# Second half of the gating at steps 1 and 2 of the next chunk; norms and input statistics at other steps

## The chip, the cores and the metric

The kernel runs on one core of a Trainium2 chip. The metric is the device time of one execution in microseconds. Engines run side by side, each takes its own instructions in order, and they meet only at semaphores: TensorE (PE, with PEld for its weight loads), VectorE (DVE), ScalarE (ACT), GpSimd (POOL), and SyncE (SP), which issues most of the transfers.

## The reference

For `x` of 8 x 64 x 56 x 56 floats:

```
x = x + conv3x3(groupnorm32(x))
t = tokens of x                       # 3136 tokens of 64 channels for each image
t = t + softmax(q k^T / 8) v          # q, k, v are linear maps of layernorm(t)
l = layernorm(t) @ gate_w + gate_b    # 16 experts
top 2 of softmax(l), renormalised     # two gates for each token
t = t + sum over the two experts of gate * (silu(h w1) * (h w2)) w3, h = layernorm(t)
```

## The kernel before, in words

**Tiling.** An image is cut into 7 chunks of 448 tokens, 56 chunks in all, numbered n = 0 to 55; c = n mod 7 is the place in the image. The queries of a chunk meet all 3136 keys of its image in 25 steps of 128 keys. One pass through `body(at)` is one chunk: each engine walks the same 25 steps and at each step issues its share. The order is written out by hand in tables of step numbers; there is no planner. So a step is a place in each engine's own queue and no moment in time: an engine can be steps behind another, held only by semaphores.

**What a chunk holds.** In each step PE makes the scores (L1463, L1464, two matmuls), ACT their exponential (L951), and PE weighs the values with it in groups of four or five (L1475: five pairs of halves at step 1, four at 5, 9, 13, 17, 21). Beside that three other chunks are in work: the one a whole image ahead ("pre": group norm, convolution L1501, tokens, layer norm `norm1`/`apply1`, keys), the one just attended ("post", chunk n-1: output projection, `attended`, layer norm `norm2`/`apply2`, transposes L1547, gate matmul L1554, `logits`, gating), and experts of an earlier image ("experts", `gated` on DVE).

**The maxima.** PE also computes the next chunk's scores once, only for their maxima ("passes", L1435, 21 or 28 of them in a chunk), and DVE reduces each (L1116). The passes go round two PSUM buffers, so pass m waits until DVE has reduced pass m-2 (`max_red`). The table `max_passes` gives most steps one pass, steps 2 (and 3 for c = 6) two where c is 1, 3, 5 or 6, and steps 0 to 4 two each where c is 0. DVE issues the reduces of a step first, then the entries of `STEPS` in order, then the combines, the experts, and `next_queries` (q_b, step 9).

**The gating** of the post chunk has two halves. The first: transposes (11), gate matmul (12), `logits` (13: add of the bias and four top-8 searches). The second: `picked` (step 16: four index searches L1183, one subtract L1184), `compared` (17: L1189 and two compares L1191), `gate_exp` on ACT (17, L894), `gates` (18: L1201 to L1203). Where c = 0 (and at chunk 53) the image's or group's routing starts at step 18 of the same chunk and needs all picks.

**Input statistics.** For the group norm of the image two ahead, SP loads a chunk of `x` into the only buffer `x_st` (L594, two halves, semaphore `x_st_in`), as the first thing in its `body` for the chunk, after the last things of the body before: the store of the experts' results (L620), which waits for the last result of that chunk (`fy_ready`). DVE waits for `x_st_in` and takes the statistics (`stats`, L1039) at step 9. This runs for n = 0 to 41; in the last chunk of an image the aggregation L1045 follows.

**POOL** makes both `rstd` powers at its steps `NORM2_AT` and `NORM1_AT`, between indirect DMAs.

Of the kernel before, what the change touches and what calls it, by code (L numbers as in the profile page):

```python
# [16 lines left out]
CHUNKS = TOKENS // CHUNK  # L17
# [59 lines left out]
def fx_loads(e, part):  # L77
# [21 lines left out]
COMBINES = {4: ((1, 0),), 5: ((0, 1), (1, 2)), 6: ((0, 3), (1, 4)), 8: ((0, 5), (1, 6))}  # L99
COMBINES_LAST = {4: ((1, 0),), 5: ((0, 1), (1, 2)), 6: ((0, 3), (1, 4)), 7: ((0, 5),), 8: ((0, 6),)}  # L100
GATHERS = {4: (0, 1), 5: (2, 3), 6: (4, 5), 7: (6,)}
NORM2_AT, NORM1_AT, RSTD_AT = 7, 11, 14
MOVES_AT = {4: (13, 16, 19, 22), 8: (1, 4, 8, 12, 15, 17, 19, 21), 9: (1, 4, 8, 11, 13, 15, 17, 19, 21),
            10: (0, 2, 4, 8, 12, 14, 16, 18, 20, 22)}
MOVES_AT_STORED = (4, 8, 12, 14, 16, 18, 20, 22)
# [7 lines left out]
SCATTERS_LAST = {GROUPS[-2].routed_at + 1: (0, 1), GROUPS[-2].routed_at + 2: (2, 3), ALL: (4, 5, 6)}  # L113
LAST = LATE + 2 * CHUNKS - 1
CONV_AT = 5
STEPS = [(4, "pre", "normed"), (4, "post", "attended"), (4, "post", "residual"), (6, "pre", "convolved"),
         (6, "post", "norm2"), (7, "pre", "tokens"), (8, "post", "apply2"), (9, "stats", "stats"), (10, "pre", "norm1"),
         (11, "post", "turned2"), (12, "post", "gate"), (13, "post", "logits"), (13, "stats", "mean"), (13, "stats", "deviation"),
         (14, "stats", "variance"), (14, "stats", "scale"), (14, "pre", "apply1"), (16, "post", "picked"), (17, "pre", "turned"),
         (17, "post", "compared"), (17, "post", "gate_exp"), (18, "post", "gates")]  # L120

# [64 lines left out]
def wait_past(engine, sem, value):  # L188

    if value > 0:  # L190
        engine.wait_ge(sem, value)
# [19 lines left out]
class At:  # L211
# [111 lines left out]
    def chunk(self, stage):  # L323

        if stage == "experts":
            return GROUP_SLICES[self.index("experts")][1]
        return self.index(stage) - CHUNKS * self.batch(stage)


def alone_pairs(at):  # L330
# [5 lines left out]
def expert_steps(at):  # L336

    if at.beside:
        return [(i, name, at, pair) for i, _, name, pair in EXPERT_STEPS
                if at.active("experts") and pair < at.pair_count()]  # L340
    if not at.active("experts"):
        return []
    steps, pairs = [], alone_pairs(at)
    here = [k for k, (mine, _) in enumerate(pairs) if mine.n == at.n]
    if here[-1] == len(pairs) - 1:
        here += [len(pairs) + k for k in range(3)]
    for place, k in enumerate(here):
        for name, behind in (("fx", 0), ("hidden", 1), ("gated", 1), ("down", 3), ("turn", 2)):
            if 0 <= k - behind < len(pairs):
                steps.append((at.steps() - KEY_TILES + 1 + 4 * place, name) + pairs[k - behind])  # L350
    return steps
# [13 lines left out]
def build(nc, x, conv_w, wq, bq, wk, bk, wv, bv, gate_w, gate_b, w1, w2, w3, out):  # L365
# [11 lines left out]
    with ctx:  # L377
        def sb(name, shape, dt=f32):
            return ctx.enter_context(nc.sbuf_tensor(name, shape, dt))
# [7 lines left out]
        before = sb("before", [TILE, TILE])  # L387
# [61 lines left out]
        gates = sb("gates", [TILE, 4, 2, TILES])  # L449
# [402 lines left out]
        def _(act):  # L852
# [55 lines left out]
            def expert(at, name, pair):  # L908
# [15 lines left out]
                elif name == "down":  # L924
                    act.wait_ge(s["y_done"], f + 1)
                    if pair == 0:
# [3 lines left out]
                                 (ps_z if at.beside else ps_m[1])[:, 0:2 * CHANNELS].rearrange("p (t c) -> p t c", c=CHANNELS),  # L930
                                 ACT.Copy, scale=0.5).then_inc(s["fy_ready"], 1)

            events = {"normed": normed, "tokens": tokens, "turned": turned,
                      "turned2": turned2, "gate_exp": gate_exp}

            def next_queries(n):
                act.wait_ge(s["q_done"], n + 1)
                a.activation(q_a[:, n % CHUNKS % QUERIES, :], ps_y[:, 0:CHUNK], ACT.Copy)\
                    .then_inc(s["qa_ready"], 1)

            def next_shift(n):
                wait_apart(act, s["shiftT_done"], n + 1)
                a.activation(q_a[0:1, n % CHUNKS % QUERIES, :], ps_y[0:1, 0:CHUNK], ACT.Copy)\
                    .then_inc(s["shift_ready"], 1)

            def body(at):
                experts = expert_steps(at)
                for i in range(at.steps()):
                    if at.attends:
                        act.wait_ge(s["s_done"], at.n * KEY_TILES + (i + 1))  # L950
                        a.activation(prob[(at.n * KEY_TILES + i) % PROBS][:], ps_s[(at.n * KEY_TILES + i) % 2][:, 0:CHUNK], ACT.Exp).then_inc(s["p_ready"], 1)  # L951
                    if i == Z_AFTER and at.active("post"):

                        act.wait_ge(s["pv_done"], (at.index("post") + 1) * KEY_TILES)
                        wait_past(act, s["outp_done"], at.index("post"))
                        a.activation(z_s[:], ps_o[:, 0:CHUNK], ACT.Copy).then_inc(s["z_ready"], 1)
                    for step, stage, name in STEPS:
                        if step == i and name in events and at.active(stage):
                            events[name](at)
                    for place, k in at.combines():  # L960
                        if i == at.combined_at(place):
                            combined(k)
                    for step, name, mine, pair in experts:
                        if step == i:
                            expert(mine, name, pair)
                    if i == at.ask_at and at.asks:
                        next_queries(at.n + 2)
                    if i == at.max_to + 1 and at.ahead:
                        next_shift(at.n + 1)
# [29 lines left out]
        def _(dve):  # L999
            v = nc.vector  # L1000

            def last_of_image(event):

                return lambda at: event(at.u + 2) if at.static and at.c == CHUNKS - 1 else None
# [288 lines left out]
            def combine(k):  # L1293
# [5 lines left out]
                for m in range(TOP):  # L1299
# [6 lines left out]

            events = {"normed": border, "convolved": conv, "norm1": norm1,
                      "apply1": apply1, "residual": attended, "norm2": norm2, "apply2": apply2,
                      "logits": logits, "picked": picked, "compared": compared,
                      "gates": gates_of,  # L1310
                      "stats": stats, "deviation": last_of_image(deviation), "scale": last_of_image(scale)}

            def body(at):
                b, coded = at.routes, CODES_AT.get(at.n)
                routes = b is not None
                codes_at = {4: 0, 5: 1, 9: 2, 13: 3, 17: 4} if coded is not None else {}
                maxima_at = max_passes(at) if at.ahead else ()
                codes_link = Link(dve, s["rt_link"], (coded or 0) * 25 + 12)
                link = Link(dve, s["rt_link"], (b or 0) * 25)
                experts = expert_steps(at)  # L1320
                for i in range(at.steps()):
                    for n, m in maxima_at[i] if at.ahead else ():
                        reduces(n, (m,))
                    for step, stage, name in STEPS:
                        if step == i and name in events and at.active(stage):
                            events[name](at)
                    for place, k in at.combines():
                        if i == at.combine_at(place):
                            combine(k)
                    for step, name, mine, pair in experts:  # L1330
                        if step == i:
                            expert(mine, name, pair)
                    if i in codes_at:
                        route_experts(coded, codes_link, codes_at[i])
                    if i == 3 and 1 <= at.n <= EXPERTS // 2:

                        expert_weights(at.n - 1)
                    if i == at.ask_at + 1 and at.asks:
                        next_queries(at.n + 2)
                    if i == at.max_to and at.ahead:  # L1340
                        max_total(at.n + 1)
                    if routes and i == 18:
                        route_pick(b)
                    if routes and i == 19:
                        route_total(b, link)
                    if routes and i == 20:
                        route_rank(b, link)
                    if routes and i == 21:
                        route_runs(b, link)
                        route_start(b, link)  # L1350
                    if routes and i == 22:
                        route_slot(b, link, 0)
                    if routes and i == 23:
                        route_slot(b, link, 1)
                    if routes and i == 24:
                        route_slots(b, link)
                assert not routes or link.count == 12, link.count
# [54 lines left out]
        def _(pe):  # L1412
# [243 lines left out]
            def body(at):  # L1656
# [18 lines left out]
                for i in range(at.steps()):  # L1675
# [16 lines left out]
                    if i == at.ask_at and at.asks:  # L1692
                        queries(at.n + 2, *divmod(at.n + 2, CHUNKS))
                    for step, stage, name in STEPS:
                        if step == i and name in events and at.active(stage):
# [90 lines left out]
```

## Time and profile before

| | us |
|---|---|
| median of 3 runs | 2696.83 (2693.95 to 2698.46) |
| the profiled execution | 2697.52 |
| its span, first to last instruction | 2695.8 |
| its mean granted TensorE clock | 0.963 |

A row of a timeline has the start, the busy time, the engine, the line and the tiles written and read; `x3` is three such instructions in a row, and what stands in brackets is idle time before and what ended it. The chunks spoken of below start, by their first score matmul, at 1084.79 (chunk 24), 1126.37 (25), 1259.91 (28), 1392.15 (31) and 1433.68 (32); chunk 33 starts at 1476.9. An image takes about 306.7 us in the middle of the run.

### The profile page before, as it was taken

The numbers are of one execution on the slowest core, as the hardware profiler recorded it, in microseconds if no ns is written. First come the engines' busy times: TensorE is split into PE (matmuls) and PEld (weight loads), VectorE is DVE, ScalarE is ACT, GpSimd is POOL, SyncE is SP. The second block draws the span as 40 slices with busy tenths as digits, with TensorE's granted clock in tenths as the row PEclk, the third lists the DMA queues.
The fourth block names the chain that finished last, engine by engine and source line by source line (L and its number), as shares of the span: only waits on it lengthen the run. The fifth ranks groups of instructions, "written<-read, shape, count | busy, mean of one in ns | idle before, by whom it ended". The sixth has DMA issues, their size and how long they took to land.

```text
span 2695.8 us, 46824 instructions
## 1 busy us (share of the span) xinstructions
PE 2443.3 (91%) x13821; PEld 1635.1 (61%) x13821; DVE 1804.3 (67%) x5891; ACT 1298.4 (48%) x2986; POOL 1012.8 (38%) x1097
## 2 busy tenths in 40 slices
PE   5899989999999999999999999999999999997773
PEld 3455555566666666666666666666666666664662
DVE  5576676667776777677766776677767777774432
ACT  2344444455554555455555555455555555453542
POOL 2022005300344424442444324443344324465765
PEclk8899999999999999999999999999999999997875
DMA  3143101111112222222222122222222112222442
GB/s 75 27 92 78 43 21 46 47 41 39 52 50 62 48 58 62 59 55 53 57 57 62 48 51 68 56 54 54 54 54 55 45 42 59 55 54 65 122 95 51
DMA packets 226560, 152.98 MB, mean 57 GB/s; under 512 B 100240, under 2 KB 216720, under 8 KB 226320
## 3 DMA queue, kind: packets, MB, share of 16 engines
q1 hardware_dynamic: 190880, 98.26, 14.0%
q0 software_dynamic: 31456, 48.03, 7.5%
q10 hardware_dynamic: 3984, 3.70, 0.5%
q8 instruction: 125, 2.05, 0.3%
q14 instruction: 115, 0.94, 0.1%
HBM read 83.92 MB, written 65.27 MB: 55 GB/s over the span
## 4 chain that ended last, share of the span: by engine, by line
PE 62%; DVE 17%; issue 5%; POOL 2%; ACT 1%; DMA 0%; POOLq 0%; ACTq 0%; DVEq 0%
PE ps_o L1475 17%; PE ps_m L1435 8%; PE ps_s L1463 7%; PE ps_s L1464 6%; DVE max_part L1116 5%; PE ps_z L1501 4%; PE ps_z L1648 3%; PE ps_x L1634 3%; PE ps_z L1623 2%; PE ps_s L1634 1%; PE ps_y L1538 1%; PE ps_y L1554 1%; DVE v_s L1029 1%; PE ps_y L1449 1%; PE ps_y L1562 1%
## 5 line engine op out<-in xcount | busy, mean ns | idle before, releaser
L1116 DVE TENSOR_REDUCE max_part<-ps_m 128x1 f32<-128x448 f32 x1400 | 845.1, 620 | 607.4 <-PE ps_m L1435 595.2
L951 ACT ACTIVATE prob<-ps_s 128x448 f32<-128x448 f32 x1400 | 758.7, 545 | 579.2 <-PE ps_s L1464 549.8
L1475 PE MATMUL ps_o<-prob,v_s 128*64 128x448 f32 x2800 | 622.1, 552 | 0.0
L1435 PE MATMUL ps_m<-k_a,q_a 128*128 128x448 f32 (+3 forms) x1600 | 540.1, 365 | 64.5 <-DVE max_part L1116 55.3
L1463 PE MATMUL ps_s<-q_a,k_a 128*128 128x448 f32 x1400 | 586.5, 419 | 2.4 <-ACT prob L951 0.8
L780 POOL DMA_INDIRECT got<-sorted_y,slot x448 | 425.6, 950 | 423.5 <-PE ps_s L1464 219.5
L759 POOL DMA_INDIRECT sorted_x<-xn,slot x448 | 426.3, 952 | 324.8 <-PE ps_s L1464 168.8
L1464 PE MATMUL ps_s<-q_b,k_a 128*128 128x448 f32 x1400 | 512.0, 366 | 0.0
L1435 PEld LDWEIGHTS ps_m<-k_a,q_a 128*128 128x128 f32 (+1 forms) x1600 | 294.7, 188 | 162.8 <-DVE max_part L1116 131.5
L1475 PEld LDWEIGHTS ps_o<-prob,v_s 128*64 128x64 f32 x2800 | 178.7, 136 | 274.1 <-issue 250.7
L1463 PEld LDWEIGHTS ps_s<-q_a,k_a 128*128 128x128 f32 x1400 | 265.3, 189 | 107.8 <-issue 84.6
L798 POOL TENSOR_TENSOR ln_s<-ln_s,minus_half 112x4 f32<-112x4 f32 x56 | 58.1, 1038 | 601.7 <-DVE ln_s L1025 560.4
L1464 PEld LDWEIGHTS ps_s<-q_b,k_a 128*128 128x128 f32 x1400 | 266.6, 190 | 7.7 <-issue 2.8
L794 POOL TENSOR_TENSOR ln_s<-ln_s,minus_half 112x4 f32<-112x4 f32 x56 | 57.5, 1026 | 281.0 <-DVE ln_s L1025 196.7
L1648 PEld LDWEIGHTS ps_z<-w3s,hidT 128*128 128x128 f32 x828 | 109.7, 190 | 85.2 <-issue 75.4
L929 ACT ACTIVATE fy<-ps_z 128x128 f32<-128x128 f32 x207 | 56.5, 273 | 207.8 <-PE ps_z L1648 207.8
L1501 PE MATMUL ps_z<-xg,wT 128*64 128x224 f32 x1344 | 146.6, 370 | 1.0 <-DVE xg L1069 1.0
L1501 PEld LDWEIGHTS ps_z<-xg,wT 128*64 128x64 f32 x1344 | 100.3, 143 | 56.2 <-issue 25.8
L1648 PE MATMUL ps_z<-w3s,hidT 128*128 x828 | 129.2, 279 | 2.5 <-ACT hidT L923 2.4
L918 ACT ACTIVATE th<-ps_x 128x256 f32<-128x256 f32 x207 | 79.4, 384 | 92.4 <-PE ps_x L1634 86.0
L1634 PE MATMUL ps_x<-w_hi,fxT 128*128 x414 | 122.3, 317 | 1.0 <-ACT fxT L914 0.6
L914 ACT ACTIVATE fxT<-ps_z 128x256 fp32r<-128x256 f32 x264 | 102.1, 387 | 39.9 <-PE ps_z L1623 26.4
(186 smaller groups left out, 2971.1 us busy)
## 6 DMA issues: line engine op xcount, KB each, us to landing
fx<-sorted_x SPq DMA_DIRECT2D x43, 384.0 KB
sorted_y<-fy SPq DMA_DIRECT2D x42, 320.0 KB
xh<-in_x SPq DMA_DIRECT2D x96, 126.0 KB
fx<-sorted_x SPq DMA_DIRECT2D x47, 256.0 KB
sorted_x<-fy POOLq DMA_DIRECT2D x28, 320.0 KB, 6.0
sorted_x<-xn,slot POOLq DMA_INDIRECT x448
got<-sorted_y,slot POOLq DMA_INDIRECT x448
x_now<-in_x SPq DMA_DIRECT2D x112, 56.0 KB
```

Of the source, the lines that this page charges most:

```text
L759: g.indirect_dma_start(out=sorted_x[b % 2], out_offset=bass.IndirectOffsetOnAxis(ap=slot[:, b % 4, k, c * PER + j:c * PER + j + 1], axis=0 ...
L780: g.indirect_dma_start(out=got[k % 2][m][:, j, :], out_offset=None, in_=sorted_y[b % 2][0:GROUPS[group_of(k)].room * SLOTS], in_offset=bas ...
L914: a.activation(fxT[:, f % 2, :], ps_z[:, 0:2 * SLOTS], ACT.Copy).then_inc(s["fxT_ready"], 1)
L951: a.activation(prob[(at.n * KEY_TILES + i) % PROBS][:], ps_s[(at.n * KEY_TILES + i) % 2][:, 0:CHUNK], ACT.Exp).then_inc(s["p_ready"], 1)
L1116: v.tensor_reduce(max_part[n % 2][0:here.stop - here.start, j, kb:kb + 1], ps_m[(passes_before(n) + m) % 2][0:here.stop - here.start, 0:CH ...
L1435: done = t.matmul(ps_m[before % 2][0:here.stop - here.start, first:last], q_a[:].rearrange("p a c -> p (a c)")[:, here], keys, start=True, ...
L1463: t.matmul(ps_s[t_of % 2][:, 0:CHUNK], k_a[p][:, keys], high, start=True, stop=False)
L1464: t.matmul(ps_s[t_of % 2][:, 0:CHUNK], k_a[p][:, keys], low, start=False, stop=True).then_inc(s["s_done"], 1)
L1475: t.matmul(ps_o[side:side + CHANNELS, 0:CHUNK], v_s[u % 2][:, i, :], prob[(n * KEY_TILES + i) % PROBS][:], start=(i < 2), stop=(i >= KEY_T ...
L1501: last = t.matmul(ps_z[64 * half:64 * half + 64, 0:CHUNK // 2], wT[:, down, k, :], xg[:, top:top + ROWS // 2, k:k + SIDE], start=(down == ...
L1634: last = t.matmul((ps_x if at.beside else ps_s[f % 2])[:, j * 2 * HIDDEN:(j + 1) * 2 * HIDDEN], fxT[:, f % 2, j * SLOTS:(j + 1) * SLOTS], ...
L1648: last = t.matmul((ps_z if at.beside else ps_m[1])[:, j * CHANNELS:(j + 1) * CHANNELS], hidT[:, j * SLOTS:(j + 1) * SLOTS], weights[f, j][ ...
```

## The change

It is one of order alone: `picked`, `compared`, `gate_exp` and `gates` leave `STEPS`, and `pick_steps(at)` gives them to steps 1 and 2 of the next chunk, except for the chunk whose body starts a routing, which keeps them at 16 to 18. `stats` goes from step 9 to 1, `norm2` from 6 to 5, `apply2` from 8 to 9, `norm1` from 10 to 11, and POOL's powers from 7 and 11 to 6 and 12. In a step the picks come after the entries of `STEPS`, so at step 1 `stats` is ahead of `picked`.

```diff
-NORM2_AT, NORM1_AT, RSTD_AT = 7, 11, 14
+NORM2_AT, NORM1_AT, RSTD_AT = 6, 12, 14
...
-STEPS = [(4, "pre", "normed"), (4, "post", "attended"), (4, "post", "residual"), (6, "pre", "convolved"),
-         (6, "post", "norm2"), (7, "pre", "tokens"), (8, "post", "apply2"), (9, "stats", "stats"), (10, "pre", "norm1"),
+STEPS = [(1, "stats", "stats"), (4, "pre", "normed"), (4, "post", "attended"), (4, "post", "residual"), (5, "post", "norm2"),
+         (6, "pre", "convolved"), (7, "pre", "tokens"), (9, "post", "apply2"), (11, "pre", "norm1"),
          (11, "post", "turned2"), (12, "post", "gate"), (13, "post", "logits"), (13, "stats", "mean"), (13, "stats", "deviation"),
-         (14, "stats", "variance"), (14, "stats", "scale"), (14, "pre", "apply1"), (16, "post", "picked"), (17, "pre", "turned"),
-         (17, "post", "compared"), (17, "post", "gate_exp"), (18, "post", "gates")]
+         (14, "stats", "variance"), (14, "stats", "scale"), (14, "pre", "apply1"), (17, "pre", "turned")]
+PICK_STEPS = [(1, "picked"), (1, "compared"), (2, "gate_exp"), (2, "gates")]
+PICK_STEPS_ROUTED = [(16, "picked"), (17, "compared"), (17, "gate_exp"), (18, "gates")]
...
+def pick_steps(at):
+
+    before = At(*divmod(at.n - 1, CHUNKS))
+    out = [(step, name, before) for step, name in PICK_STEPS if before.active("post") and before.routes is None]
+    return out + [(step, name, at) for step, name in PICK_STEPS_ROUTED if at.active("post") and at.routes is not None]
...
+                    for step, name, mine in pick_steps(at):
+                        if step == i and name in pick_events:
+                            pick_events[name](mine)
```

The last loop stands in DVE's `body` behind the loop over `STEPS`; ACT's `body` has the same for `gate_exp`.

## Rows read from the trace of the kernel before

**Rows 1.** The page: busy time, share and instructions of each engine.
```profile
PE 2443.3 (91%) x13821; PEld 1635.1 (61%) x13821; DVE 1804.3 (67%) x5891; ACT 1298.4 (48%) x2986; POOL 1012.8 (38%) x1097
```

**Rows 2.** Waits: engine, line, waited for; us in total, times, longest.
```profile
PEld ps_m L1435 <- DVE max_part L1116: 131.5, 191, 2.3
...
PE ps_m L1435 <- DVE max_part L1116: 55.3, 92, 1.9
...
PE ps_y L1547 <- DVE q_b L1108: 13.8, 27, 1.6
```

**Rows 3.** Chain of waits, start of chunk 31: start, us, what.
```profile
1396.84 0.64 DVE max_part L1116
...
1397.52 0.47 PE ps_m L1435
```

**Rows 4.** Timeline, starts of chunks 31, 32 and 28: DVE's reduces, PE's passes.
```profile
1396.84 1.81 DVE L1116 TENSOR_REDUCE max_part<-ps_m 128x1 f32<-128x448 f32 x3 [2.58 <-PE ps_m L1435]
...
1438.40 1.24 DVE L1116 TENSOR_REDUCE max_part<-ps_m 128x1 f32<-128x448 f32 x2 [2.58 <-PE ps_m L1435]
...
1439.43 0.36 PE L1435 MATMUL ps_m<-k_a,q_a 128*128 128x448 f32 x1
...
1264.79 2.99 DVE L1116 TENSOR_REDUCE max_part<-ps_m 128x1 f32<-128x448 f32 x5 [2.18 <-PE ps_m L1435]
...
1267.62 0.69 PE L1435 MATMUL ps_m<-k_a,q_a 128*128 128x448 f32 x2
```

**Rows 5.** Timeline of SP: the `x_st` loads for chunks 31, 32 and 4.
```profile
1393.29 1.38 SPq L594 DMA_DIRECT2D x_st<-in_x  x2
...
1435.60 1.12 SPq L594 DMA_DIRECT2D x_st<-in_x  x2
...
223.54 1.19 SPq L594 DMA_DIRECT2D x_st<-in_x  x2
```

**Rows 6.** DMA, GB/s in 40 slices of 0.2 us, from 1392.15 and 1433.68.
```profile
GB/s 0 0 0 0 251 36 0 9 216 221 218 215 220 196 196 311 164 94 220 179 40 0 0 72 215 0 0 0 0 0 0 41 0 0 0 0 0 0 0 0
...
GB/s 0 0 0 0 0 0 23 141 159 233 323 351 346 333 318 323 344 318 284 291 296 220 140 126 155 169 174 15 0 0 0 0 0 0 0 0 0 0 0 0
```

**Rows 7.** Timeline of DVE in chunk 25: first and last of `picked`, then `compared`.
```profile
1156.47 0.08 DVE L1183 MATCH_VALUE_LOAD top_i<-top,logit 112x8 f32 x1
...
1157.06 0.17 DVE L1184 TENSOR_TENSOR gate_d<-top 112x4 f32<-112x4 f32 x1
...
1157.72 0.23 DVE L1189 CAST top_f<-top_i 112x8 f32<-112x8 uint32 x1
1157.98 0.41 DVE L1191 TENSOR_TENSOR pick<-expert_f,top_f 112x64 f32<-112x64 f32 x2
```

**Rows 8.** Timeline of DVE and PE, chunk 32, steps 8 to 11.
```profile
1449.80 1.06 DVE L1029 TENSOR_SCALAR ln_c<-t_now,ln_mv,ln_s 112x64 f32<-112x64 f32 x4 [0.19 <-POOL ln_s L798]
...
1451.23 0.42 DVE L1165 TENSOR_TENSOR xn<-ln_c,xn 112x256 fp32r<-112x256 f32 x1
...
1452.10 0.38 DVE L1039 BATCH_NORM_STATS2 gn_stats<-x_st 128x6 f32<-128x224 f32 x1
...
1453.18 0.61 DVE L1108 TENSOR_TENSOR q_b<-ps_y,q_a 128x448 fp32r<-128x448 f32 x1
...
1450.21 0.36 PE L1435 MATMUL ps_m<-k_a,q_a 128*128 128x448 f32 x1
...
1454.13 0.57 PE L1547 MATMUL ps_y<-ident,xn 112*128 112x112 f32 x4
```

**Rows 9.** Timeline of DVE and PE, steps 18 to 21 of chunks 32 and 31.
```profile
1467.91 0.16 DVE L1201 TENSOR_SCALAR gate_d<-gate_e 112x4 f32<-112x4 f32 x1
...
1468.39 0.76 DVE L1300 TENSOR_TENSOR got<-got,gates 112x256 f32<-112x256 f32 x2
...
1470.66 0.47 PE L1435 MATMUL ps_m<-k_a,q_a 128*128 128x448 f32 x1 [0.55 <-DVE max_part L1116]
...
1428.06 0.54 PE L1435 MATMUL ps_m<-k_a,q_a 128*128 128x112 f32 x2 [0.20 <-DVE max_part L1116]
```

More of the change, by code:

```diff
@@ L931, in expert @@
                                  ACT.Copy, scale=0.5).then_inc(s["fy_ready"], 1)
-            events = {"normed": normed, "tokens": tokens, "turned": turned,
-                      "turned2": turned2, "gate_exp": gate_exp}
+            events = {"normed": normed, "tokens": tokens, "turned": turned, "turned2": turned2}
             def next_queries(n):
@@ L959, in body @@
                             events[name](at)
+                    for step, name, mine in pick_steps(at):
+                        if step == i and name == "gate_exp":
+                            gate_exp(mine)
                     for place, k in at.combines():
@@ L1308, in _ @@
                       "apply1": apply1, "residual": attended, "norm2": norm2, "apply2": apply2,
-                      "logits": logits, "picked": picked, "compared": compared,
-                      "gates": gates_of,
-                      "stats": stats, "deviation": last_of_image(deviation), "scale": last_of_image(scale)}
+                      "logits": logits, "stats": stats, "deviation": last_of_image(deviation), "scale": last_of_image(scale)}
+            pick_events = {"picked": picked, "compared": compared, "gates": gates_of}
             def body(at):
@@ L1326, in body @@
                             events[name](at)
+                    for step, name, mine in pick_steps(at):
+                        if step == i and name in pick_events:
+                            pick_events[name](mine)
                     for place, k in at.combines():
```

## The prediction, made before the changed kernel ran

> **What bounds the kernel.** I read the page first. PE is busy for 91% of the span and DVE for 67% [rows 1], so the bound is PE, and a change of DVE's order can matter only where DVE makes PE wait. The waits show where that is: PE and its weight loads waited for the reduces of the maxima (two views of largely the same waits, 55 us on PE itself), and for `q_b` 13.8 us [rows 2]. Everything moved here is on DVE, or on ACT for one small operation. So the sum is: which pass of maxima comes later, which earlier, by how much, in how many chunks. The chain of waits at the start of chunk 31 shows the mechanism: a DVE reduce ends at 1397.48 and the next pass on PE starts at 1397.52 [rows 3]. That pass needs the reduce two passes back, and PE takes its work in order, so all behind it waits too, the scores included.
>
> **The new front of a chunk: the input statistics.** They used to be asked for at step 9, where the data had long been there. Now DVE asks at step 1, and every later item of DVE, the reduces of step 2 first, stands behind that wait. When does the load land? SP issues it at 1393.29 to 1394.67 in chunk 31 [rows 5], 1.1 us after the chunk's start, because the store of the experts' results is before it. The data traffic of that stretch ends in the slice up to 1396.35 [rows 6]; what follows from 1396.75 is another transfer (SP issues no more there). So the load's last bytes come 1.7 us after its issue ends and 4.2 us after the chunk's start, and DVE can begin at about 1396.6. In chunk 32 the issue is later (1435.60 to 1436.72 [rows 5]), behind the loads of expert inputs: with the same 1.7 it lands at 1438.4, and the traffic, a later load with it, ends at 1439.2 [rows 6]. I take 1438.9. The load for chunk 4 went out at 223.54, 18.6 us before its chunk [rows 5]: while SP is not held by the store of the results before, the wait costs nothing. By the code and the start of the expert work (chunk 11 is the first held), 31 chunks wait: n = 11 to 41.
>
> The price in chunk 31 (c = 3), from there on by durations: statistics 0.38 [rows 8]; `picked` 1157.23 - 1156.47 = 0.76; `compared` 0.67 [rows 7]; DVE's items overlap by some 0.1 each, so 1.6 together. That gives 1398.2, and the first reduce of step 2 (0.6) ends at 1398.8. Before it ended at 1397.48 [rows 3, 4]. PE's pass and all of PE behind it come 1.3 to 1.4 us later. DVE idled for 2.58 us before those reduces [rows 4], but that hole ends at 1396.84: the picks alone would fit in it, behind a wait until 1396.6 they don't. By c:
> - c = 3 and 5: 1.4 each, 4 and 5 chunks, 12.6.
> - c = 2 and 4 have one pass at steps 2 and 3, so the pass held is that of step 4. In chunk 32 it started at 1439.43 [rows 4]; new, 1438.9 + 0.1 + 1.6 + 0.6 = 1441.2, 1.8 later (1.2 with the early landing, 2.1 with the late). Five chunks, 9.0. For c = 2, landing as in chunk 31, 1.3 each, four chunks, 5.2.
> - c = 6: as c = 3, and the aggregation (0.35 and a semaphore) stands there too; 1.9 each, five chunks, 9.5.
> - c = 1: no picks (its predecessor keeps them), only 0.38 behind the landing: 0.2 each, 0.8.
> - c = 0: passes come two a step, and DVE reduces without a pause until the step's end: five in a row, 1264.79 to 1267.78 [rows 4]. The first of these is step 1's, so no landing is waited for; but there is no hole either. Statistics and picks (1.6) and `gates` (0.5, [rows 9]) stand in full ahead of the reduces that PE's passes at 1267.62 need: 2.1 each in five chunks, 1.7 in the two without statistics (n = 42, 49), 13.9.
>
> Sum at the front: 51 us. Bounds: 41 with landings 0.3 earlier and chunk 32's early one, 66 if DVE gets going 0.3 later and PE, after a stall, issues its next waits 0.2 slower. The chunks before 11 and after 41 (c not 0) pay nothing: there picks of 1.3 us go into a hole of 2.58 [rows 4].
>
> What the Trainium skill has on this: "DMA: Bandwidth & Descriptors", section "Anatomy of one DMA", gives a fixed cost of about 2.0 us and bytes over 436 GB/s. For the second half of the load (57 KB, issued from 1394.0) that makes 1396.1; the trace has data until 1396.35. By the page's figure the front would be some 8 us cheaper in sum, and the time about 2740. The same page ("Issuing engines are not separate DMA queues") says that transfers share 16 engines whoever issues them; chunk 32's later end agrees, and it speaks against a step-1 deadline right behind a store of 320 KB.
>
> **Norm 2 earlier, apply 2 later.** `norm2` (about 1.2 us) moves from behind x_conv into DVE's idle time while PE does the convolution: nothing gained at once, since POOL's power and `apply2` were done in time; its cover is the hole between `gated` at step 5 and the reduce of step 6, 1.9 us in chunk 31. `apply2` now waits behind step 9's reduce. In chunk 32 PE's pass of step 9 starts at 1450.21, the reduce runs 1450.4 to 1451.0; `apply2` takes 1.85 (1449.80 to 1451.65), `gated` 0.75, q_b 0.55 net: q_b ends at 1454.2, against 1453.79 before; the transposes at 1454.13 stand 0.34 behind it [rows 8]. Without its cover, `apply2` before the reduce, the order costs 0.4. I take 0.4 for c = 1, 4 and 5, 0.3 for 0, 2 and 3, none for 6: 2.1 an image, 17 over eight. Bounds: 0, if DVE's idle time before `apply2` (0.19) and the missing statistics pay for it, and 0.6 a chunk, 33.
>
> **Norm 1 at 11.** 1.25 us later on DVE, POOL's power at 12; `apply1` at 14 sits behind the reduce of step 14 as before, several us later. Nothing; bounds 0 and 0.3 a chunk if POOL is inside an indirect DMA. The two POOL steps pass no queue item that a consumer asks for at once: nothing.
>
> **What the old places give back.** At step 18, `gates` runs right ahead of the combine; then come reduces for which PE idles: in chunk 32 `gates` 1467.91 to 1468.47, the combine, the reduces, and PE's pass at 1470.66 after 0.55 idle [rows 9]. Without `gates` 0.55 comes back, in chunks with a combine at step 18 (c = 4, 5, 6 and 1, from n = 18 on): 23, 12.7 us. In c = 3 the digits of the expert codes stand there: PE waits at 1428.06, 0.20 by its row and more in its weight load [rows 9]; 0.8 in six chunks, 4.8. The large wait at step 17 is behind `apply1`, ahead of `picked`: it stays. Together 17 (bounds 10 and 25).
>
> **Sum.** 51 + 17 - 17 = +51 us on the profiled 2697.52: 2748.5. The median of the runs is 0.7 below the profiled one, so 2748.
>
> **The rivals.**
> A. *The landing is hidden*: the load is there when DVE asks, or the hole before the reduces takes it all. Against it [rows 5, 6]; for it that chunks before 11 have it so. Then only c = 0 pays (14): 14 + 17 - 17 = +14, 2711.
> B. *Faster: the hole takes everything, c = 0 too, and q_b has slack.* One mechanism: DVE idles a third of the time [rows 1] and 2.58 us at exactly this place [rows 4], and only the relief at steps 18 to 21 reaches PE: -17, 2680. It decides if landing plus 1.6 is before 1396.84 in chunk 31, that is a landing by 1395.2, 1.2 us before the data's end, and if the two-pass steps of c = 0 have a spare 2 us; five reduces in a row say no.
> C. *Slower still: `gate_exp` holds ACT.* It stands at step 2 ahead of step 3's exponential and waits for `picked`. If this comes through to PE behind the late reduces, 0.2 to 0.4 in some 45 chunks: +13, 2762. Against it: PE is itself late there and asks for that exponential only at step 5.
> D. *Nothing shifts*, gains and losses cancel: +-5, 2697; needs half of the front.
>
> **Chances.** Forecast 0.65, A 0.12, B 0.07, C 0.13, D 0.03. The range reaches from A's time to somewhat above C's, which also holds the bounds of front, apply 2 and relief taken together: 2711 to 2775. By 0.2% (5.4 us, about what a measurement can tell here) it is slower with 0.90 (forecast, A, C), the same 0.03, faster 0.07.
>
> **What would show it.** In the changed trace: in chunks 11 to 41, L1039 a few us after the chunk's start with DVE idle before it, ended by the DMA; the pass at step 3 or 4 waiting for L1116, PE's and its weight loads' waits for L1116 up by about 50 us in total; chunk lengths up by 1.2 to 2 us for c = 2 to 6 and by 2 for c = 0 (less what step 21 gives back); in chunks 43 to 48 no loss but at step 11; L1547's wait for q_b up by about 15 us; PE's wait at step 21 smaller by 0.5. Wrong it would be if L1039 starts without a wait, if PE's pass behind it isn't held, or if c = 0 keeps its length.

## The result, and the profile after the change

| | before | after |
|---|---|---|
| median of 4 runs each | 2696.07 (2693.95 to 2698.46) | 2788.32 (2782.09 to 2798.46) |
| the profiled execution | 2697.52 | 2798.46 |
| its span | 2695.8 | 2796.7 |
| its mean granted TensorE clock | 0.963 | 0.947 |

The changed kernel is slower: ratio 1.0346, 95% interval 1.0312 to 1.0379, that is 92 us where 51 were forecast, and outside the range. The profiled execution is the longest of its four; the other three had a clock of 0.950 to 0.954, so it shows the loss at its largest.

In `kernel.py` after the change the pass of the maxima is L1447, the reduce L1126, `stats` L1049, `picked` L1193, the `x_st` load L602, the values' matmul L1487, q_b L1118, the transposes L1559.

The page after, its line of busy times and its chain of waits by engine and line, answers to [rows 1]:

```profile
PE 2488.8 (89%) x13821; PEld 1666.2 (60%) x13821; DVE 1803.8 (64%) x5891; ACT 1301.7 (47%) x2986; POOL 1009.0 (36%) x1097
...
PE ps_o L1487 14%; PE ps_m L1447 8%; PE ps_s L1475 7%; PE ps_s L1476 6%; PE ps_x L1646 3%; DVE max_part L1126 3%; PE ps_z L1513 3%; PE ps_z L1660 3%; DMA x_st<-in_x 3%; PE ps_y L1550 2%; PE ps_z L1635 2%; DVE ln_c L1039 2%; PE ps_y L1566 1%; DVE v_s L1039 1%; PE ps_s L1646 1%
```

The same 13821 matmuls keep PE busy 45 us longer: a part of them ran slower. The load of `x_st`, unseen before, is 3% of the chain. The waits after (us in total, times, longest), for [rows 2]:

```profile
PEld ps_m L1447 <- DVE max_part L1126: 174.1, 193, 3.7
...
PE ps_m L1447 <- DVE max_part L1126: 100.5, 104, 3.4
...
DVE gn_stats L1049 <- DMA x_st<-in_x: 77.5, 27, 5.7
...
PE ps_y L1559 <- DVE q_b L1118: 23.7, 45, 1.4
```

PE's own wait for the reduces rose by 45 us, its weight loads' by 43, the wait for q_b by 10. DVE waits 77.5 us for the new deadline, in 27 chunks: of the 31 from 11 to 41, the four with c = 0 don't wait. What these waits leave out is the slower matmuls.

Steps can be compared one by one, since each starts with a score matmul. The first matmul of each step, taken from both traces, gives the length of every step of every chunk; the differences after minus before, summed over 56 chunks:

| steps | us |
|---|---|
| 0 to 2 | -0.1 |
| 3, 4, 5 | +42.4, +49.5, +17.6 |
| 6 to 10 | +3.1 |
| 11 | +10.2 |
| 12 to 19 | +1.6 |
| 20, 21 | -5.7, -16.9 |
| 22 to 24 | +1.1 |
| ahead of chunk 0 | -4.1 |
| behind chunk 55 | +2.1 |

The line ahead of chunk 0 is a delay before the first chunk that comes and goes between executions (-4.1 or about 0 in the kernels below). The chunks 0 to 10 sum to +1, 11 to 41 to +96, 42 to 55 to +5, as the wait's place says. The front, steps 3 to 5, holds 109.5.

**Chunk 31** starts at 1452.03 in the new trace. Its timeline, for [rows 3, 4]:

```profile
1453.17 1.39 SPq L602 DMA_DIRECT2D x_st<-in_x  x2
...
1456.58 0.39 DVE L1049 BATCH_NORM_STATS2 gn_stats<-x_st 128x6 f32<-128x224 f32 x1 [2.43 <-DMA x_st<-in_x]
...
1458.23 1.15 DVE L1126 TENSOR_REDUCE max_part<-ps_m 128x1 f32<-128x448 f32 x2
...
1458.91 0.47 PE L1447 MATMUL ps_m<-k_a,q_a 128*128 128x448 f32 x1 [1.61 <-DVE max_part L1126]
...
1462.51 1.73 PE L1487 MATMUL ps_o<-prob,v_s 128*64 128x448 f32 x8
```

That is the forecast's chunk: statistics 4.55 us after the chunk's start (4.45 forecast), the pass at +6.88, where it was at +5.37 before [rows 3]: 1.5 later, 1.3 to 1.4 forecast.

**Chunk 32** starts at 1494.48, and isn't the forecast's. The chain of waits there (start, us, what):

```profile
1493.28 2.28 DMA sorted_x<-xn,slot
...
1495.68 0.36 SPq L591
...
1496.13 0.50 SPq L591
...
1496.83 0.36 SPq L628
...
1497.28 0.47 SPq L602
...
1497.80 3.59 DMA x_st<-in_x
...
1501.42 0.39 DVE gn_stats L1049
...
1503.08 0.64 DVE max_part L1126
...
1503.76 0.74 PE ps_m L1447
```

Read it from the top. The last scatter of POOL (`sorted_x`) lands 1.1 us into the chunk; the loads of expert inputs (L591) wait for it, on SP's queue the store L628 and then the `x_st` loads stand behind them. So `x_st` is asked for at +2.80 (+1.92 before [rows 5]), lands at +6.9 (+5.2 forecast), and the pass of step 4 starts at +9.28 (+5.75 before [rows 4]). And that pass took 0.74 us, not 0.36: two rows of the timeline, and three stretches with engines' busy time, granted clock (PEclk), DMA share and GB/s:

```profile
1503.76 0.74 PE L1447 MATMUL ps_m<-k_a,q_a 128*128 128x448 f32 x1 [3.36 <-DVE max_part L1126]
...
1507.92 2.98 PE L1487 MATMUL ps_o<-prob,v_s 128*64 128x448 f32 x8
```
```profile
1458.90:1463.50 4.60, 4.29 (x27) 3.16 (x29) 3.98 (x14) 2.55 (x5) 1.62 (x2) 1.00 0.05 16
1503.70:1510.50 6.80, 6.74 (x24) 4.52 (x26) 4.89 (x23) 1.76 (x4) 0.57 (x1) 0.50 0.08 21
1510.50:1515.00 4.50, 4.10 (x32) 2.58 (x28) 1.03 (x4) 1.09 (x2) 0.47 (x1) 1.00 0.00 0
```

Behind the 1.61 us stall of chunk 31 the clock stayed at 1.00, 2.4 GHz. Behind the 3.36 us stall of chunk 32 it was 0.50, 1.2 GHz, for 6.8 us, and eight matmuls of the values took 2.98 us instead of 1.73. Chunk 32 is the longest of its kind: in chunks 18, 25 and 39 (c = 4 too) the statistics start at +6.1 to +6.4, not +6.9, and the pass stalls for 2.6 to 2.8 us. The trace of the granted clock has 18 such stretches behind stalls of the front in chunks 7 to 40, 3.4 or 6.8 us each, and one of 3.4 in chunk 53. In chunks 6 to 54 there are 105.8 us at half clock; in the profile of before 3.4. By the largest gap between PE's matmuls ahead of each: of the 10 chunks with a gap above 2 us at the front all were followed by one, of the 16 with 1.3 to 2 us eight, of those with less one (chunk 53, 1.0 us). So the same chunk type costs differently. For c = 3, over steps 3 to 5: chunks 31 and 38, with no half clock, lose 1.5 us; chunk 17 (3.4 us of it) 2.8; chunk 24 (6.8) 4.6.

**The rest.** For [rows 8], steps 9 to 11 of chunk 32; for [rows 9], the pass of step 20 in chunk 31 and that of step 21 in chunk 32; for chunk 28 of [rows 4], the start of chunk 28 (c = 0, from 1315.44):

```profile
1520.07 0.43 DVE L1175 TENSOR_TENSOR xn<-ln_c,xn 112x256 fp32r<-112x256 f32 x1
...
1521.20 0.62 DVE L1118 TENSOR_TENSOR q_b<-ps_y,q_a 128x448 fp32r<-128x448 f32 x1
...
1522.07 0.57 PE L1559 MATMUL ps_y<-ident,xn 112*128 112x112 f32 x4 [0.39 <-DVE q_b L1118]
...
1489.29 0.43 PE L1447 MATMUL ps_m<-k_a,q_a 128*128 128x112 f32 x2
...
1538.10 0.47 PE L1447 MATMUL ps_m<-k_a,q_a 128*128 128x448 f32 x1
...
1323.19 1.00 PE L1447 MATMUL ps_m<-k_a,q_a 128*128 128x448 f32 x2 [1.31 <-DVE max_part L1126]
```

The transposes wait 0.39 us for q_b (0.4 forecast for c = 4). The passes of [rows 9] that waited 0.20 and 0.55 wait no more. c = 0 stalls although it doesn't wait for a landing: the pass that is held stood at +6.27 before and starts at +7.75 now. It comes two passes before the pair at 1267.62 by which the prediction priced this chunk.

### The profile page after: what moved, and what is told of

Read it like the earlier page. It is cut to its first block, busy times and chain, and to the rows that moved or that the text cites. A ratio compares the mean times of both kernels' runs of the same rounds, so it can differ in the third digit from the quotient of the medians.

```text
span 2796.7 us, 46785 instructions
## 1 busy us (share of the span) xinstructions
PE 2488.8 (89%) x13821; PEld 1666.2 (60%) x13821; DVE 1803.8 (64%) x5891; ACT 1301.7 (47%) x2986; POOL 1009.0 (36%) x1097
## 4 chain that ended last, share of the span: by engine, by line
PE 57%; DVE 16%; issue 6%; DMA 4%; POOL 2%; SPq 1%; ACT 1%; POOLq 0%; ACTq 0%; DVEq 0%
PE ps_o L1487 14%; PE ps_m L1447 8%; PE ps_s L1475 7%; PE ps_s L1476 6%; PE ps_x L1646 3%; DVE max_part L1126 3%; PE ps_z L1513 3%; PE ps_z L1660 3%; DMA x_st<-in_x 3%; PE ps_y L1550 2%; PE ps_z L1635 2%; DVE ln_c L1039 2%; PE ps_y L1566 1%; DVE v_s L1039 1%; PE ps_s L1646 1%
## 5 line engine op out<-in xcount | busy, mean ns | idle before, releaser
L1126 DVE TENSOR_REDUCE max_part<-ps_m 128x1 f32<-128x448 f32 x1400 | 846.8, 620 | 634.1 <-PE ps_m L1447 620.0
L1447 PE MATMUL ps_m<-k_a,q_a 128*128 128x448 f32 (+3 forms) x1600 | 547.8, 369 | 107.1 <-DVE max_part L1126 100.5
L1487 PE MATMUL ps_o<-prob,v_s 128*64 128x448 f32 x2800 | 633.6, 561 | 0.0
L1447 PEld LDWEIGHTS ps_m<-k_a,q_a 128*128 128x128 f32 (+1 forms) x1600 | 300.2, 190 | 206.0 <-DVE max_part L1126 174.1
L1487 PEld LDWEIGHTS ps_o<-prob,v_s 128*64 128x64 f32 x2800 | 181.3, 138 | 282.2 <-issue 248.4
L1646 PE MATMUL ps_x<-w_hi,fxT 128*128 x414 | 128.4, 330 | 0.8 <-ACT fxT L922 0.6
```

Of the source, the lines that this page charges most:

```text
L1126: v.tensor_reduce(max_part[n % 2][0:here.stop - here.start, j, kb:kb + 1], ps_m[(passes_before(n) + m) % 2][0:here.stop - here.start, 0:CH ...
L1447: done = t.matmul(ps_m[before % 2][0:here.stop - here.start, first:last], q_a[:].rearrange("p a c -> p (a c)")[:, here], keys, start=True, ...
L1487: t.matmul(ps_o[side:side + CHANNELS, 0:CHUNK], v_s[u % 2][:, i, :], prob[(n * KEY_TILES + i) % PROBS][:], start=(i < 2), stop=(i >= KEY_T ...
L1646: last = t.matmul((ps_x if at.beside else ps_s[f % 2])[:, j * 2 * HIDDEN:(j + 1) * 2 * HIDDEN], fxT[:, f % 2, j * SLOTS:(j + 1) * SLOTS], ...
```

## The experiments

All on one chip per group, each beside runs of the kernel before (medians 2699.07, 2699.75 and 2698.72 in the three groups). The changed kernel itself wasn't run again in these groups, so a comparison with its 2788.32 goes across groups; the ratios go by the runs of before beside each kernel. Two theories stood against the forecast's single one: that half clock after the stalls is a cost of its own, and that the parts of the change don't add up. "Front" is steps 3 to 5, summed over the profiled execution as in the table above. Half clock is that of chunks 6 to 54; in chunk 55 there are 3.4 us more in the kernel before and in b_stats1, and 10.2 in a_norms_back, b_picks, b_picks_c0 and b_best.

| kernel | median, us | ratio to before (95%) | front | step 11 | half clock, chunks 6 to 54, us |
|---|---|---|---|---|---|
| after | 2788.32 | 1.0346 (1.0312, 1.0379) | +109.5 | +10.2 | 105.8 |
| a_fill | 2761.48 | 1.0226 (1.0208, 1.0245) | +66.0 | +8.8 | 20.5 |
| a_fill_half | 2764.78 | 1.0243 (1.0225, 1.026) | +74.0 | +9.0 | 30.7 |
| a_stats9 | 2728.29 | 1.0107 (1.0086, 1.0127) | +19.2 | +24.9 | 20.5 |
| a_xst2 | 2720.70 | 1.0084 (1.0067, 1.0101) | +24.6 | +10.1 | 20.5 |
| a_norms_back | 2762.43 | 1.0232 (1.0185, 1.028) | +86.5 | -9.5 | 64.9 |
| b_stats1 | 2702.36 | 1.0014 (1.0005, 1.0024) | +9.9 | -11.4 | 17.1 |
| b_picks | 2706.48 | 1.0026 (1.0016, 1.0036) | +19.4 | +1.7 | 17.1 |
| b_norms | 2728.26 | 1.0109 (1.0092, 1.0126) | +0.4 | +23.5 | 10.2 |
| b_picks_c0 | 2690.43 | 0.9972 (0.9962, 0.9981) | +5.7 | +2.3 | 13.7 |
| b_best | 2680.09 | 0.9933 (0.992, 0.9946) | +7.0 | -9.4 | 10.2 |
| b_best_n2 | 2670.77 | 0.9893 (0.9878, 0.9908) | +6.0 | -20.8 | 20.5 |

**a_fill: is half clock a cost of its own?** The changed kernel with matmuls that feed nothing, put where PE stalls:

```diff
+STALLS = {0: (3, 6), 1: (9, 0), 2: (4, 6), 3: (3, 7), 4: (4, 14), 5: (3, 8), 6: (3, 8)}   # c: (step, how many)
+def filler(at, many):
+    if many:
+        pe.wait_ge(s["z_ready"], at.n)
+    for _ in range(many):
+        t.matmul(ps_o[:, 0:CHUNK], k_a[at.u % 2][:, 0:128], q_a[:, at.c % QUERIES, :], start=True, stop=True)
...
+                        if 11 <= at.n < 42 and i == STALLS[at.c][0]:
+                            filler(at, STALLS[at.c][1])
```

> The changed kernel with 6 to 14 additional matmuls of 448 columns on PE, ahead of the pass that waits, at step 3 or 4 of chunks 11 to 41 (not c = 1); their output is overwritten and nobody reads it. They fill the time in which PE would idle. Theory 2 (about 45 us of the loss is PE at 1.2 GHz for 3 to 7 us after a stall of over 2 us): the granted clock stays at 2.4 GHz there, and the time falls from 2788 to 2735 to 2755. Rival (the low clock costs nothing, since PE would wait for DVE anyway, or doesn't come from the stall): 2780 to 2800, or the stretches at half clock stay.

Measured 2761.48, 27 us below the changed kernel with more work in it, and 6 us above the range expected. Against the runs of before beside each, the loss fell from 92 to 62 us, that is by 30. Chunk 32 starts at 1472.44; its filler and its pass, then the same 12 us of chunk 32 by clock, here and without filler:

```profile
1478.20 3.01 PE L1471 MATMUL ps_o<-q_a,k_a 128*128 128x448 f32 x14
1478.79 0.40 DVE L1049 BATCH_NORM_STATS2 gn_stats<-x_st 128x6 f32<-128x224 f32 x1 [4.21 <-DMA x_st<-in_x]
...
1481.13 0.47 PE L1447 MATMUL ps_m<-k_a,q_a 128*128 128x448 f32 x1
```
```profile
1472.44:1484.44 12.00, 12.00 (x62) 8.43 (x64) 6.71 (x30) 5.53 (x12) 1.91 (x2) 1.00 0.36 96
```
```profile
1494.50:1506.50 12.00, 8.64 (x39) 6.04 (x40) 5.43 (x24) 4.58 (x10) 1.94 (x2) 0.88 0.36 94
```

The clock stays at 1.00, no stretch of half clock is left at the front, and PE issued 62 matmuls in the 12 us, 14 of them filler, instead of 39. DVE waits for the landing all the same. The front falls from 109.5 to 66.0: 43.5 us of the profiled execution. 40.1 of them lie in the 27 chunks that have filler; in chunks 7 and 53, which have none, 4.3 went because no half clock followed their stalls in this execution. In the medians the gain is 27 to 30; the profiled execution of the changed kernel had the lowest clock of its four. Chance isn't the cause: all four executions of a_fill have a clock of 0.962 to 0.965, all four of the changed kernel 0.947 to 0.954.

The Trainium skill, "TensorE: Matmul & The Clock Gate", section "HAM oscillation", describes a matmul kernel that waits for a transfer between groups, falls to 1.2 GHz each time, and loses half of the time spent so. By that the 85.3 us that filler removed (105.8 - 20.5) would be worth 43, an estimate. The trace agrees in the main: the spans of the two profiled executions differ by 36.3 us. At the front alone 99.0 us of half clock went, by that rule worth 49.5, and the front fell by 43.5, somewhat less than half.

**a_fill_half**: how little will do?

```diff
-STALLS = {0: (3, 6), 1: (9, 0), 2: (4, 6), 3: (3, 7), 4: (4, 14), 5: (3, 8), 6: (3, 8)}
+STALLS = {0: (3, 3), 1: (9, 0), 2: (4, 3), 3: (3, 4), 4: (4, 7), 5: (3, 4), 6: (3, 4)}
```

> The changed kernel with half of the additional matmuls (3 or 4, 7 for c = 4). Theory 2: they shorten PE's idle stretch to 1 us or so, which may be enough to keep 2.4 GHz; then the time is that of the full number or a few us less (2752 to 2762), since none of them outlasts the stall. Rival (the clock falls with any idle time behind step 3): 2775 or more, with stretches at half clock as in the changed kernel.

2764.78, a little above the range expected: half the filler keeps the clock up in most chunks (it fell at the front in chunks 7, 25, 27 and 40) and gives no time over the whole filler. So the filler itself did not cost the rest of a_fill's front.

**a_xst2: is it the landing or the place?** Two buffers, loads a chunk earlier, statistics still at step 1:

```diff
-        x_st = sb("x_st", [128, CHUNK // 2])
+        x_st = [sb(f"x_st{p}", [128, CHUNK // 2]) for p in range(2)]
...
-                if at.active("stats"):
-                    load_stats(at)
+                ahead = At(*divmod(at.n + 1, CHUNKS))
+                if ahead.active("stats"):
+                    load_stats(ahead)
```

> The changed kernel with two buffers for the input load, each load issued one chunk earlier; the statistics stay at step 1. Theory 1: what costs is the landing and not the place; DVE does 0.38 us of statistics in its idle time, so the time is that of the kernel with the statistics at step 9 or a little less (q_b earlier by 0.3 in c = 1 to 5): 2690 to 2702. Rival (the place costs, since statistics and picks together fill DVE's hole): 2720 or more.

2720.70, 19 us above the upper end but 68 below the changed kernel. By its number it falls to the rival (2720 or more); the steps say otherwise. The waits no longer have `x_st`, and in chunk 32 (from 1441.52) the statistics start at +2.06:

```profile
PE ps_m L1447 <- DVE max_part L1126: 53.8, 92, 1.9
```
```profile
1443.58 0.38 DVE L1049 BATCH_NORM_STATS2 gn_stats<-x_st 128x6 f32<-128x224 f32 x1
...
1447.28 0.36 PE L1447 MATMUL ps_m<-k_a,q_a 128*128 128x448 f32 x1
```

The pass of step 4 starts at +5.76, where it was before (+5.75). With the data there, statistics and picks cost at most 0.25 us a chunk for c = 1 to 6 between chunks 12 and 41 (0.44 in chunk 26): they fit in DVE's hole. What is left of the front, 24.6, is mostly c = 0: 17.8, of it 1.9 in a chunk at full clock, and 4.1 and 4.7 in chunks 7 and 35, where half clock followed. Another 3.3 is chunks 11 and 53. In chunk 11 PE waits 1.5 us for the load of the expert input `fx`, which also goes out later in the chunk (+3.25; +0.23 before). In chunk 53 the passes come two a step as in c = 0 (`max_passes` does that for a chunk that starts a routing).

**a_stats9** puts the statistics back to step 9, behind `apply2`:

```diff
-STEPS = [(1, "stats", "stats"), (4, "pre", "normed"), ... (9, "post", "apply2"), (11, "pre", "norm1"),
+STEPS = [(4, "pre", "normed"), ... (9, "post", "apply2"), (9, "stats", "stats"), (11, "pre", "norm1"),
```

> The changed kernel with one entry moved back: the input statistics at step 9. Theory 1 (the wait for the input load at step 1 holds DVE, and the PE stalls that follow bring the clock down to 1.2 GHz in chunks 11 to 41): the front loss of c = 1 to 6 goes, c = 0 keeps about 1.7 us each; step 11 costs some 15 us more than in the kernel before, steps 20 and 21 give back 22; 2696 + 12 + 15 - 22 = 2701, and no stretch at half clock outside c = 0. Rival (the picks at steps 1 and 2 are themselves too much for DVE): a front loss of over 1 us in most chunks stays and the time is above 2730.

2728.29, 27 above. The front (19) was expected at 12: c = 0 costs 1.6 a chunk and 4.3 in chunk 7. Step 11 was expected at 15 and is 25. Half clock outside c = 0, where none was expected, is there in chunks 31, 41 and 53, 13.7 us. In chunk 32 (from 1453.33) the statistics stand between `apply2` and q_b, and the transposes wait twice as long:

```profile
1472.49 0.39 DVE L1049 BATCH_NORM_STATS2 gn_stats<-x_st 128x6 f32<-128x224 f32 x1
...
1473.57 0.61 DVE L1118 TENSOR_TENSOR q_b<-ps_y,q_a 128x448 fp32r<-128x448 f32 x1
...
1474.53 0.57 PE L1559 MATMUL ps_y<-ident,xn 112*128 112x112 f32 x4 [0.78 <-DVE q_b L1118]
```

**b_norms** is the kernel before with `norm2`, `apply2`, `norm1` and POOL's powers alone at their new steps:

```diff
-NORM2_AT, NORM1_AT, RSTD_AT = 7, 11, 14
+NORM2_AT, NORM1_AT, RSTD_AT = 6, 12, 14
...
+STEPS = [... (5, "post", "norm2"), ... (9, "post", "apply2"), (9, "stats", "stats"), (11, "pre", "norm1"),
```

> The kernel before with only the norms, apply 2 and POOL's powers at their new steps; the statistics stay at 9, behind apply 2 now. Theory: q_b comes 0.7 us later and the transposes at step 11 wait for it in nearly every chunk (the changed kernel with the statistics at 9 lost 25 us at step 11): +22 to +27, 2719 to 2726. Rival (that loss needs the picks' new place too): 2700 to 2708.

2728.26, 2 us above the range. The loss is step 11, 23.5 us: 0.6 to 0.8 in most chunks from 11 to 48, at most 0.3 before. Its wait for q_b, and then that of b_stats1:

```profile
PE ps_y L1547 <- DVE q_b L1108: 38.8, 53, 1.5
```
```profile
PE ps_y L1547 <- DVE q_b L1108: 6.8, 11, 1.5
```

**b_stats1** and **b_picks** are the kernel before with one part alone:

```diff
-... (8, "post", "apply2"), (9, "stats", "stats"), (10, "pre", "norm1"),
+STEPS = [(1, "stats", "stats"), ...
```

> The kernel before with one entry moved: the input statistics at step 1, picks where they were. If the losses of statistics and picks add up, this has most of the front loss: 2740 to 2760. If, as theory 1 has it, the landing alone eats only DVE's idle time and the picks behind it turn it into a stall, 31 chunks lose 0.2 to 0.4 us, and c = 4 about 1: 2703 to 2712.

```diff
+PICK_STEPS = [(1, "picked"), (1, "compared"), (2, "gate_exp"), (2, "gates")]   # stats and norms stay
```

> The kernel before with only the picks moved to steps 1 and 2 of the next chunk; statistics, norms and POOL as before. Theory 1: the picks fit DVE's idle time where no load is waited for; the loss is at c = 0 alone (1.6 us in 7 chunks, 11), the relief at steps 20 and 21 is 21: 2685 to 2692, that is faster than before. Rival (picks at 1 and 2 load DVE whatever the statistics do): over 2700.

b_stats1, 2702.36, is 0.6 us below its range, and not by its theory alone: the front loses 9.9, about as expected, but step 11 gains 11.4 and steps 12 to 19 lose 8.0, neither of which was in the expectation. b_picks, 2706.48, missed by 14 us. Its profiled execution (2698.29) was the fastest of ten, so its rows show 8 us less than its median; the others had clocks of 0.958 to 0.962 against its 0.964. In these rows: relief at steps 20 and 21 (22.5) as in the changed kernel, but the front lost 19.4, of it 13.8 in c = 0 (1.6 a chunk, 4.1 in chunk 7), and steps 12 to 19 lost 6.8, partly after half clock at step 17 of c = 6. In b_stats1 the wait for the landing is there as in the changed kernel; the timeline of chunk 32 (from 1436.46):

```profile
1438.40 1.13 SPq L594 DMA_DIRECT2D x_st<-in_x  x2
...
1442.08 0.40 DVE L1039 BATCH_NORM_STATS2 gn_stats<-x_st 128x6 f32<-128x224 f32 x1 [3.47 <-DMA x_st<-in_x]
```

Issue at +1.94 and statistics at +5.62: without the picks' move the load is a microsecond earlier than in the changed kernel. In b_picks, which has the relief, the load is issued at +2.82. So it is the relief, 0.9 us at the end of the chunk before, that brings the chunk's start closer to POOL's last scatter and makes `x_st` late in c = 4. The other 0.5 of the 1.3 us between the two starts of the statistics is the load itself, 3.68 us from issue to statistics here and 4.14 in the changed kernel; what made it longer isn't separated.

**a_norms_back** takes the norms back and leaves picks and statistics:

```diff
-NORM2_AT, NORM1_AT, RSTD_AT = 6, 12, 14
+NORM2_AT, NORM1_AT, RSTD_AT = 7, 11, 14
...
+STEPS = [(1, "stats", "stats"), ... (6, "post", "norm2"), (7, "pre", "tokens"), (8, "post", "apply2"), (10, "pre", "norm1"),
```

> The changed kernel with norms, apply 2 and POOL's powers back at their old steps. Theory: step 11 gives back its 10 us and, since the statistics are no longer between apply 2 and q_b, some 8 us more; the front loss and its half clock stay: 2768 to 2780. Rival (the norms carry a large part of the unexplained loss): under 2750.

2762.43 (2746.55 to 2772.59, the widest spread of all), 6 us below what was expected, with 64.9 us of half clock where the changed kernel had 105.8. Its front is 86.5, that of its two parts alone 9.9 and 19.4: **the parts don't add**. Landing alone or picks alone fit into most of the hole; one behind the other they don't, and then the stalls are long enough that the clock fell.

**Versions that keep the gain.** b_picks_c0 is b_picks with c = 0 taking its picks at steps 5 and 6; b_best has the statistics at 5 as well; b_best_n2 has `norm2` at 5, POOL's power at 6, the statistics at 7 and `apply2` at 8 as before:

```diff
+PICK_STEPS_FIRST = [(5, "picked"), (5, "compared"), (5, "gate_exp"), (6, "gates")]   # where c is 0
...
-STEPS = [... (4, "post", "residual"), (6, "pre", "convolved"), (6, "post", "norm2"), (7, "pre", "tokens"), (8, "post", "apply2"), (9, "stats", "stats"),
+STEPS = [... (4, "post", "residual"), (5, "post", "norm2"), (6, "pre", "convolved"), (7, "pre", "tokens"), (7, "stats", "stats"), (8, "post", "apply2"),
```

> As the kernel with only the picks moved, but the picks that fell to steps 1 and 2 of the chunks with c = 0 are at 5 and 6, in DVE's idle time while PE does the convolution. Theory: the 11 us at c = 0 go and only the relief is left: 2674 to 2681. Rival (DVE has no slack at 5 and 6 of c = 0 either): as the kernel without that, 2685 to 2692.

> The kernel with only the picks moved (c = 0 takes them at 5 and 6), and the input statistics at step 5, where the load has landed a microsecond or more before and DVE idles. The kernel with the statistics at 1 alone got 11 us back at step 11. Theory: the same here without a wait: 2690 - 10 = 2680, 2677 to 2684. Rival (step 5 is full, or step 11 is held by something else by now): 2688 to 2695.

> As the one before, but norm 2 (and POOL's power for it) at step 5 as in the changed kernel, and the statistics at 7; apply 2 stays at 8. Theory: apply 2 no longer waits 0.2 us for POOL, so q_b comes a little earlier where step 11 still waits: 2674 to 2682. Rival (norm 2 at 5 delays the expert's second operation and with it the convolution's end): 2684 or more.

b_picks_c0 has 2690.43, 9 above its range and in that of its rival. But c = 0 pays nothing at the front any more, so not the rival but steps 12 to 19 (+8.6) account for it, with half clock at step 17 again. b_best has 2680.09 (hit), b_best_n2 2670.77 (3 us better than expected): 1.07% below the kernel before, 4.2% below the changed one. In b_best_n2 the statistics stand at step 7, long after the landing, and q_b is hardly waited for: its page and its wait,

```profile
PE 2435.5 (91%) x13821; PEld 1638.9 (61%) x13821; DVE 1804.8 (68%) x5891; ACT 1300.3 (49%) x2986; POOL 1011.2 (38%) x1097
```
```profile
PE ps_y L1560 <- DVE q_b L1119: 1.4, 5, 0.3
```

against 13.8 us before [rows 2].

## Why the prediction missed, by its steps

The sum for the profiled execution was 2748.5; it took 2798.5. By terms, forecast and measured:

| term | forecast | measured |
|---|---|---|
| front, steps 3 to 5 | +51 | +109.5 |
| step 11, q_b | +17 | +10.2 |
| relief, steps 20 and 21 | -17 | -22.6 |
| not forecast: steps 6 to 10, 12 to 19, 22 to 24, 0 to 2 | 0 | +5.7 |
| ahead of chunk 0, behind chunk 55 | 0 | -2.0 |

The half clock stands in the first line: no term of the forecast was for it.

**The step that failed is the front's price**, "Sum at the front: 51 us. Bounds: 41 ... 66": it measured 109.5. Its mechanism is in the trace: the statistics wait at step 1 for a landing, ended by the DMA, and the pass behind the reduces of that step is held (a_xst2 takes the wait away and 68 us with it). Its size was wrong for two reasons:

1. *Half clock, 43 us of the profiled execution, 27 to 30 of the median* (a_fill). The forecast priced a stall at its own length. It had nothing on what PE's clock does after it, though its sum itself put PE idle for one to two microseconds more in most chunks from 11 on. With that priced, the front would have been some 15 us off, not 58.
2. *The landing of c = 4.* Forecast 1.8 in each of five chunks; without half clock (a_fill) it is 2.9 to 3.0 in four, and 4.6 in chunk 11. The forecast took SP's issue times from the trace of before as they stood, and counted the relief as a pure gain. The relief moves the chunk's start closer to POOL's scatters, and the load starts 0.9 us later in the chunk, in chunk 11 2.2 us later (+4.03; +1.82 before). There PE also waits 1.2 us (1.3 in a_fill) for the expert input `fx`, late for the same reason; the forecast had no such term.

The front by the place in the image, us over all chunks of a place:

| c | forecast | after | a_fill |
|---|---|---|---|
| 0 | 13.9 | 19.2 | 12.6 |
| 1 | 0.8 | 2.2 | 2.2 |
| 2 | 5.2 | 5.9 | 5.2 |
| 3 | 5.6 | 10.8 | 5.6 |
| 4 | 9.0 | 34.2 | 19.5 |
| 5 | 7.0 | 21.0 | 10.5 |
| 6 | 9.5 | 16.3 | 10.5 |

At full clock the forecast's prices hold for c = 0, 2, 3 and 6. What remains is c = 4 (10.5: four chunks at 1.2 above the forecast, chunk 11 at 2.8, and chunks 46 and 53 at 2.9 together, which wait for no `x_st`; in chunk 46 PE waits 1.1 us for `fx`, in this execution alone) and c = 5 (3.5). There chunks 26 and 33 lose 2.8 each: their load is issued at +1.13 as in chunk 40, but the statistics start at +5.8, not +4.7. The landing of one and the same load varies by a microsecond, which the forecast's single landing time for c = 5 left out.

**Right** besides: the chunks before 11 and after 41 pay at the front in c = 0 alone (chunk 53 apart, 3.2, of which 1.6 is left in a_fill; chunk 6 loses 0.4); the relief is where it was put, a little larger. **Step 11** is within its bounds, but the order of norms and q_b is worth more than the forecast saw: alone it costs 23.5 us (b_norms), and the move of the statistics away from step 9, which alone gives 11.4 back (b_stats1), is why only 10 are left. `norm1` and POOL's powers cost nothing that shows; no run moves them alone.

**The rivals.** A, the landing hidden, is what a_xst2 builds: 2711 was its time, 2720.7 is measured, with 10 us more at the front than A's 14. B, faster with everything in the hole, fails at c = 0, as forecast, and at the landing; with c = 0's picks and the statistics placed behind both, 2680 was reached (b_best), by another sum: step 11 gave 9.4 and the front kept 7.0. C, `gate_exp` holding ACT: ACT did wait for `picked` in chunk 32, but PE was held by the reduce. Where no landing is waited for, it costs nothing that shows: b_picks has `gate_exp` at step 2, and its chunks of c = 2 to 5 lose 0.12 us at most at the front (chunks 11 and 53 apart). Behind a late reduce no run separates it. All rivals, C at 2762 included, priced stalls at their length, so the range ended 13 us short of the median.

## What to carry to other kernels

Before an item is moved earlier, read when its producer lands in each kind of chunk, and add the item's length to the landing: an idle hole of 2.58 us doesn't cover 1.6 us of work that can only start at its end. A stall on the engine that bounds the kernel is to be priced with the granted clock behind it, and a gain at the end of a chunk can make a transfer late at the start of the next. Moves that are each nearly free (statistics +3, picks +7 us) cost 63 together (a_norms_back), so they are to be tried one at a time: with the picks early, and the statistics moved to where the load has long landed, the time was 2670.77.

## What the runs showed of the hardware

- The granted clock fell to 0.50 for 3.4 or 6.8 us behind gaps in PE's matmuls of 1.3 to 3.4 us at the front (once of 1.0), in a kernel that keeps PE busy for 89% of its span. It is no fixed rule of the gap: eight of 16 gaps of 1.3 to 2 us were followed by it and eight were not. The stretches come and go between executions of the same kernel, and the spread of its times (2782 to 2798 us for clocks of 0.954 to 0.947) goes with them.
- Matmuls whose results nobody reads, put into the stall, made the kernel 27 us faster (2788.32 to 2761.48).
- A load of 56 KB took 2.73 us from the issue of its second half to DVE's start in chunk 31, where the store of 320 KB went out just ahead of it, and 3.59 in chunk 32, where the loads of expert inputs stood ahead of the store:

```profile
1453.83 2.73 DMA x_st<-in_x
...
1497.80 3.59 DMA x_st<-in_x
```

Over all such loads of the changed kernel it is 2.1 to 3.8 us, 2.6 in the middle. "DMA: Bandwidth & Descriptors" of the Trainium skill, section "Anatomy of one DMA", has a fixed cost and a rate that make it 2.1 us, an estimate: that is the shortest here. The section is on transfers that GpSimd issues and these are issued by SyncE, which the prediction left out. That the traffic ahead makes a load longer fits these numbers; no run shows it by itself.

- Open: stretches of 3.4 us of half clock at step 17 of c = 6, behind the stall after `apply1`, were in none to five chunks of an execution. The stall is 1.6 to 1.9 us there in the kernel before too, whose profiled execution had none of them. They blur comparisons of a few microseconds. No kernel with a filler there was run.
